# Diagonals of B for a selective scan: four at a time on GpSimd instead of one per round on ScalarE

## The reference

```python
dt = jax.nn.softplus(dt_low @ W_dt + b_dt)
A = -jnp.exp(A_log)
def step(h, inp):
    dt_t, B_t, C_t, u_t = inp
    dA = jnp.exp(dt_t[:, :, None] * A)
    h = dA * h + (dt_t * u_t)[:, :, None] * B_t[:, None, :]
    y = jnp.einsum('bdn,bn->bd', h, C_t)
    return (h, y)
```

## Time and profile before

| | us |
|---|---|
| median of 3 runs | 1596.59 |
| lowest and highest run | 1590.95, 1600.13 |
| profiled execution | 1599.52 |
| its span, first to last instruction | 1597.7 |
| first scan instruction, end of the last (line 2107) | 333.0, 663.5 |
| VectorE busy over the span | 1068.1 |
| ScalarE busy over the span | 853.1 |
| GpSimd busy over the span | 477.2 |
| TensorE matmuls busy over the span | 1447.3 |

### The profile page before, as it was taken

The page is one execution under the profiler, slowest core; times in us unless marked ns, Lnnn a source line. Parts: engine busy times, 40 slices in busy tenths (PEclk is TensorE's granted clock), DMA queues, the critical chain, the costliest instruction groups (busy, mean ns, idle before and its releaser), DMA issues.

```text
span 1597.7 us, 20215 instructions
## 1 busy us (share of the span) xinstructions
PE 1447.3 (91%) x7408; PEld 988.6 (62%) x7420; DVE 1068.1 (67%) x1218; ACT 853.1 (53%) x1509; POOL 477.2 (30%) x140
## 2 busy tenths in 40 slices
PE   5898797689899999897999889999989999999997
PEld 3566343278797988743443433333358888888886
DVE  6996495669889898865443457777564565565655
ACT  3433456489989897641432358777733433333332
POOL 0999120059888897600211420000000000000000
PEclk7899999789999999978999989999999999999999
DMA  7110010502233111502012222344000000000000
GB/s 268 40 43 1 1 53 2 199 27 80 106 99 113 67 54 41 175 1 41 20 40 69 81 80 60 102 135 134 1 0 1 1 14 1 1 14 1 14 1 14
DMA packets 36624, 87.61 MB, mean 55 GB/s; under 512 B 8350, under 2 KB 24948, under 8 KB 32948
## 3 DMA queue, kind: packets, MB, share of 16 engines
q1 hardware_dynamic: 36532, 86.39, 16.3%
HBM read 68.10 MB, written 18.21 MB: 54 GB/s over the span
## 4 chain that ended last, share of the span: by engine, by line
PE 55%; DVE 2%; ACT 2%; issue 2%; DVEq 1%; ACTq 0%
PE ps L1424 12%; PE ps L1433 12%; PE ps L1292 4%; PE ps L1365 4%; PE ps L1159 3%; PE ps L1280 2%; PE ps L1185 2%; PE ps L1121 2%; PE ps L991 1%; PE ps L584 1%; ACT arena L1884 1%; PE ps L1334 1%; PE ps L1043 1%; PE ps L1193 1%; PE ps L1171 1%
## 5 line engine op out<-in xcount | busy, mean ns | idle before, releaser
L2567 POOL TENSOR_TENSOR arena<-arena 128x2048 f32<-128x2048 f32 x63 | 287.3, 4579 | 168.4 <-DVE arena L2107 168.2
L2107 DVE TENSOR_TENSOR_SCAN arena<-arena,ps 128x1024 f32<-128x1024 f32 x128 | 284.2, 2272 | 45.0 <-ACT arena L1727 22.4
L1727 ACT ACTIVATE arena<-arena,mam 128x511 f32<-128x511 f32 x256 | 165.9, 708 | 34.4 <-DVE arena L2107 34.4
L1884 ACT ACTIVATE arena<-ps,rho 128x512 f32<-128x512 f32 x256 | 158.9, 688 | 31.3 <-PE ps L1365 29.9
L2339 DVE TENSOR_REDUCE mxs<-ps 128x1 f32<-128x512 f32 x224 | 141.1, 684 | 44.9 <-PE ps L1280 43.0
L979 PE MATMUL ps<-early,arena 128*128 128x128 f32 x768 | 129.7, 277 | 18.2 <-DVE arena L2107 17.8
L1424 PE MATMUL ps<-early,arena 128*128 128x256 f32 x512 | 127.1, 380 | 2.9 <-DVE mam L2506 1.8
L1913 ACT ACTIVATE arena<-arena 128x256 f32<-128x256 f32 x192 | 85.5, 500 | 81.6 <-DVE arena L2510 50.3
L2547 POOL TENSOR_TENSOR arena<-arena 128x4096 f32<-128x4096 f32 x16 | 115.0, 7189 | 43.4 <-DVE arena L2026 43.4
L1715 ACT ACTIVATE arena<-arena,early 128x512 f32<-128x512 f32 x192 | 123.7, 707 | 0.1
L991 PE MATMUL ps<-early,arena 128*128 128x128 f32 x1024 | 121.5, 272 | 0.9 <-POOL arena L2567 0.7
(11 more groups left out here) (351 smaller groups left out, 2486.8 us busy)
## 6 DMA issues: line engine op xcount, KB each, us to landing
arena<-bc_scratch SPq DMA_DIRECT2D x32, 512.0 KB, 3.7
arena<-in_ffn SPq DMA_DIRECT2D x8, 1024.0 KB, 4.8
batch_scratch<-arena SPq DMA_DIRECT2D x2, 3072.0 KB, 9.1
arena<-batch_scratch SPq DMA_DIRECT2D x6, 1024.0 KB, 6.9
arena<-q_scratch SPq DMA_DIRECT2D x96, 64.0 KB, 2.2
arena<-k_scratch SPq DMA_DIRECT2D x96, 64.0 KB, 2.2
arena<-in_dec_w SPq DMA_DIRECT2D x1, 3855.0 KB, 16.1
arena<-in_cond SPq DMA_DIRECT2D x1, 3739.5 KB, 11.5
```

Of the source, the lines that this page charges most:

```text
L1727: last = act.activation(decay[:, (2 * k + h) % 3, i, 1:S], dt[b % 2][:, m, 1:S], ACT.Exp, scale=a_neg[:, m * NS + n:m * NS + n + 1])
L1884: act.activation(pt[:, j % 4, i], ps[:, 3 + (hg + n) % 3, :], ACT.Exp, scale=rho[:, 0:1]).then_inc(s_pt, 1)
L2107: dve.tensor_tensor_scan(half, view(decay[:, (2 * k + h) % 3], [[1, 2 * S]]), view(ps[:, FEED + 2 * h, :], [[1, 2 * S]]), 0.0, ALU.mult, A ...
L2567: pool.tensor_tensor(state[:, k % SLOTS], state[:, k % SLOTS], view(c_rows[:, j % 2, k % G, :], [[0, M], [1, S]]), ALU.mult).then_inc(s_hc, 1)
```

## The change

The diagonals for the last time block are made by GpSimd. A new buffer `b_diag` holds eight of them (`RING`); it takes the room of a quarter of `dub`, which needs three time blocks now. One instruction makes four diagonals (`QUARTER`): the identity, repeated four times, times four columns of B, each repeated along its row, 128x512 in all. Two such groups are made ahead of the loop, after `s_ends`; within the loop one follows the product of every fourth state, for four states that come five to eight rounds later. ScalarE makes the three products alone. TensorE waits before feed(k, 0) at k = 0 and 4 for `s_rows`, and at each later multiple of four for `s_hc` to reach k - 3, which is signalled by the product that stands behind the group in GpSimd's list.

```diff
+RING = 8
+QUARTER = RING // 2
...
-        dub, at = carve(at, 2, TILES, DI)
+        dub, at = carve(at, 2, TILES - 1, DI)
         c_rows, at = carve(at, 2, G, S)
+        b_diag, at = carve(at, RING, P)
...
                 if h == 0:
                     pe.wait_ge(s_dub, k + 1)
+                    if k % QUARTER == 0 and k < RING:
+                        pe.wait_ge(s_rows, 2 + k // QUARTER)
+                    elif k % QUARTER == 0:
+                        pe.wait_ge(s_hc, k + 1 - QUARTER)
...
                     last = pe.matmul(ps[:, FEED + m, LAST:S], duT[k // NS % 2][:, TILES - 1, m * P:(m + 1) * P],
-                                     dub[:, k % 2, TILES - 1, 0:P], start=True, stop=True)
+                                     b_diag[:, k % RING, :], start=True, stop=True)
...
                 for t in range(TILES - 1):
-                    act.activation(dub[:, k % 2, t, :], duT[b % 2][:, t, :], ACT.Copy, scale=bt[:, b, t, n:n + 1])
-                last = act.activation(dub[:, k % 2, TILES - 1, 0:P], ident, ACT.Copy, scale=bt[:, b, TILES - 1, n:n + 1])
+                    last = act.activation(dub[:, k % 2, t, :], duT[b % 2][:, t, :], ACT.Copy, scale=bt[:, b, t, n:n + 1])
                 last.then_inc(s_dub, 1)
...
+            def b_diagonals(quarter):
+                b, n = divmod(quarter * QUARTER, NS)
+                return pool.tensor_tensor(b_diag[:, n % RING:n % RING + QUARTER, :],
+                                          view(ident, [[0, QUARTER], [1, P]]),
+                                          view(bt[:, b, TILES - 1, n:n + QUARTER], [[1, QUARTER], [0, P]]), ALU.mult)
+
+            pool.wait_ge(s_ends, 1)
+            for quarter in range(2):
+                b_diagonals(quarter).then_inc(s_rows, 1)
             for k in range(B * NS - 1):
...
+                if k % QUARTER == QUARTER - 1 and k + 1 + QUARTER < B * NS:
+                    b_diagonals((k + 1) // QUARTER + 1)
```

More of the change, by code:

```diff
@@ L251, in program @@
         decay, at = carve(at, 3, 2, S)
-        dub, at = carve(at, 2, TILES, DI)
+        dub, at = carve(at, 2, TILES - 1, DI)
         c_rows, at = carve(at, 2, G, S)
+        b_diag, at = carve(at, RING, P)
         state, at = carve(at, SLOTS, M, S)
+        assert at <= ARENA
         zT = [view(hflat, [[DI, TILES], [1, DI]], b % 2 * M * S) for b in range(B)]
```

## The result

The changed kernel takes 1603.72 us (median of 15 runs, 1601.8 to 1605.61), the kernel before 1592.69 us beside it (15 runs, 1588.15 to 1600.13). The ratio on record is 1.0057 with a 95% interval of 1.0043 to 1.0070: slower by 9 us, between 7 and 11. The two medians lie 11.0 us apart and the two means 9.7, since the runs of before fall into two groups, around 1591 and around 1599, and its median jumps between them. The time is inside the range of 1594 to 1611 and on the side of the forecast of 1600.7, but the loss is more than twice the 4.15 us of its sum, and it lies at the 0.5% that the prediction drew as its line: the interval reaches to both sides of it.

The account below looks back on a forecast made before the run. Four nearly equal engine paces bound the scan, whichever comes last at each place. Terms 2.77 + 1.38 = 4.15 us made the run 1603.7, less 2.9 for the profiled execution's excess: 1600.7 us, range 1594 to 1611.

Parts of the forecast that it names:

- D, the price of a group: GpSimd's time for one 128x512 product making four diagonals, taken as 1.0 us.
- Batch 0, 3D - 0.23 = 2.77: Groups after states 3, 7 and 11 delay state 14, making the gating of batch 0 2.77 us later.
- Batches 1 and 2, D - 0.31 = 0.69 each: Groups after states 27 and 43 lie in gapless GpSimd runs with 0.31 us of room; 0.69 us each.
- Nine groups free: Groups after states 15, 19, 23, 31, 35, 39, 47, 51 and 55 were to cost 0.
- Relief of ScalarE, 0.23 once: Diagonals taken off ScalarE gain 0.23 us, once, at the end of batch 0, and nothing elsewhere.
- The signature: Trace signs in the scan: GpSimd at 4.8 us a round, more sum loads waiting for it, ScalarE idle up over 15 us.
- The hidden lag: Rival: in the scan GpSimd may lag up to seven slots, so only noise shows; 1596.6 us, chance 0.12.
- the dear product: Rival: GpSimd's new product costs 1.77 us or more; at 2.17 the run takes 1606.6 us; chance 0.10.
- The group after 55 ... 0: In the last rounds this group meets 1.04 us of GpSimd idle and VectorE has extra work; cost 0.
- After the scan TensorE runs nearly without a gap, so I let the delay through whole: Behind the scan, the whole 4.15 us delay was passed on to the span.
- 2.9 above the median of the three shown: Whole run: the profiled execution's excess over the median 1596.59 us, taken off 1603.7 to give 1600.7.
- the one of all fourteen groups: Rival: every group inside the loop lies on the path, 14 us, 1610.6 us; chance 0.08.

Follow-up runs that it names:

- after_again: The changed kernel run again with no edit, for a second trace; 1604.22 us, ratio 1.0058.
- pool_adds: Kernel before, ScalarE's diagonals kept and used, GpSimd also making the fourteen in-loop groups, which nobody reads; 1604.19 us, ratio 1.0074.
- the run with six delays: Kernel before with six small VectorE operations, each with a drain, put ahead of the gating of batch 0; 1601.98 us, ratio 1.0067.
- the run with fourteen: Kernel before with fourteen small VectorE operations, each with a drain, put ahead of the gating of batch 0; 1608.54 us, ratio 1.0084.

## Why the prediction was right, and where it was off

- **D, the price of a group.** 1.0 us by the row of line 2547. Measured: 1.04 us by itself (16 of them, 1.032 to 1.077), 1.00 from start to next start. The Trainium skill, GPSIMD Engine Reference, section 3.1, with about 2.6 cycles an element, would make it 1.11, an estimate; this run shows it some 6% shorter, and 10% by the pace.
- **Batch 0, 3D - 0.23 = 2.77.** Measured 2.76, and 6.47 at twice the size. The chain from GpSimd's product over the sum and the feed to the scan was the right one.
- **Batches 1 and 2, D - 0.31 = 0.69 each.** Measured 0.78, and 0.75 and 0.77 in `after_again`. The groups in those places took 1.07 and 1.06 us in the first trace and 1.03 in the second, which makes 0.72 to 0.76.
- **Nine groups free.** Right: nothing else moved in the changes of batch; the groups in them fill GpSimd's waits.
- **Relief of ScalarE, 0.23 once.** Measured 0.27 without groups, 0 on top of them in `pool_adds` (83.21 against 83.24): in batch 0 of the changed kernel the feed stands behind the sum and not behind ScalarE, so taking the 0.23 off the sum came out right by luck. A room of that size was there before the first group, whoever held the feed, as `pool_adds` shows: 3D less 0.27 with ScalarE's diagonals kept.
- **New waits of TensorE, and the start, 0.** The first scan starts 0.3 us earlier, and no feed is among the instructions that wait for GpSimd.
- **The signature.** GpSimd at 4.77 us a round (4.8 forecast), weight loads of the sum that wait for it 21 times instead of 3, ScalarE's waiting up by 19.6 us (over 15 forecast). The hidden lag is out by the three holes in batch 0, the dear product by its 1.04 us.
- **Where it failed: "The group after 55 ... 0", and "After the scan TensorE runs nearly without a gap, so I let the delay through whole".** The sum moved every instruction behind the scan by 4.15 us and took for granted that it would then last as long as before. The profile had rows that spoke against that: a clock of 0.83 from 680 to 760 us, and three runs that spread over 9 us. The term left out is TensorE's clock: 1.65 us in batch 3, measured in two traces of the same kernel, and some 3 us behind the scan, as far as the tables above can tell. The step "2.9 above the median of the three shown" was weak as well: with twelve more runs the median of before is 1592.69, so its trace lay 6.8 us above it, and a difference of 4.15 should have been read against a kernel that spreads like that. That 1600.7 lies only 3.0 us from the measured 1603.72 is partly luck: the start of the sum was 3.9 us too high, and the loss, 11.0 between the medians, 6.9 larger than the sum.
- **The chances.** I had 0.79 for "within 0.5%" and 0.17 for "slower by more"; the measured 0.57% lies just on the other side. With a term of 0 to +5 us for the clock, the sum of 4 to 5 us would have stood close to the bound of 8, and the two chances nearer to each other. The range held the time through its upper end, which was there for another rival, the one of all fourteen groups, and that one is refuted.

## What to carry to other kernels

Where three or four engines have nearly the same pace, ask for a moved operation which engine will be the one without a gap and who meets its results at once: there each microsecond counts in full, in the changes of stage it is free, and the relieved engine gives back only what it was last by (here 0.27 us of 18.6). To make such a move cheap, let the consumer take its input one round later: with that on both sides the move cost the scan 1.3 us instead of 4.3. And before a gain or loss under 1% is believed, take several traces of both kernels, compare their granted clocks behind the place of the change, and compare executions of like clock: here one kernel's own traces differ by 9 us in a part that the change doesn't touch.

## What the hardware showed that I had not expected

A short operation of VectorE waited for two long ones of GpSimd. In the run with six delays, the first of six copies of 128x128 (duration min/median/max in ns) took 5.76 us, not 0.23:

```profile
L2142 DVE TENSOR_SCALAR arena<-early x6: 226/228/5759, 415.1 to 422.1; 128x128 f32<-128x128 f32 x6
```

```profile
415.10 7.28 DVE L2142 TENSOR_SCALAR arena<-early 128x128 f32<-128x128 f32 x6
```

```profile
393.64 27.13 POOL L2572 TENSOR_TENSOR arena<-arena 128x2048 f32<-128x2048 f32 x6
```

It started at 415.10 and ended at 420.86; GpSimd's gapless row of products ended at 393.64 + 27.13 = 420.77. A product takes 4.52 us from start to start, so one of them ended about 416.2, and the copy waited through the end of it and the whole of the next. In the run with fourteen the first copy took 5.79 us, from 414.43 to 420.22, and the products ended at 420.13. That is why six copies made a delay of 7.4 us where 4.2 was meant. The Trainium skill, SBUF — State Buffer, section "Who interferes with whom", calls the port pair that VectorE and GpSimd share an exclusive lock; the trace agrees, and adds that the change of instruction on GpSimd did not hand it over. The DMA engines were 0.96 busy from 415 to 420 us, and I did not try them apart. The scans of the kernel itself, 2.27 us each, ran without a gap beside the same gapless products.

The second surprise is how well the low clock repeats with the schedule: both traces of after have it in the same round of batch 3 and the same 41 us in the 330 us behind the last gating, while the traces of before, whose scans repeat to 0.03 us, have between 27 and 48 us of it.
